# Layer 0 of a gated cross-attention network on one Trainium2 core: three neighbours change places in hand-ordered queues

## The reference

```python
x = x + tanh(g_xattn[0]) * L0_xattn(layernorm(x), ctx, ...)   # B=4, S=256, H=256, SC=1601, 16 heads, 8 groups, D=128
# in L0_xattn, for each of the 8 groups:
q  = _ln(fp8_linear(ln_out, wq));  k = _ln(fp8_linear(ln_out, wk));  v = fp8_linear(ln_out, wv)
qx = _ln(fp8_linear(ln_out, wqx)); kx, vx = split(ctx @ w_kv_x);      kx = _ln(kx)
core = softmax(q k^T / sqrt(D)) v;   xout = softmax(qx kx^T / sqrt(D)) vx
return fp8(concat(core, xout) / smooth) @ wproj.T * scale
x = x + tanh(g_ffn[0]) * L0_ffn(layernorm(x))                  # 8 experts, the best 2 weighted
```

## Time and profile before

| what | us |
|---|---|
| median of 3 runs (lowest, highest) | 1678.73 (1677.43, 1679.62) |
| the profiled execution, its own time | 1676.05 |
| its span | 1674.2 |
| TensorE busy | 1576.3 |
| VectorE busy | 1388.7 |
| ScalarE busy | 1387.7 |
| GpSimd busy | 1140.4 |
| mean granted clock of TensorE, share of full | 0.993 |

### The profile page before, as it was taken

How to read it: one execution, slowest core, us unless ns; L and a number is a source line. 1 busy time by engine, 2 the same in 40 slices (tenths; PEclk the granted TensorE clock), 3 DMA queues, 4 the chain that set the end, 5 groups by cost and what they waited for, 6 DMA issues and landing times.

```text
span 1674.2 us, 43879 instructions
## 1 busy us (share of the span) xinstructions
PE 1576.3 (94%) x15804; PEld 1000.5 (60%) x15996; DVE 1388.7 (83%) x3486; ACT 1387.7 (83%) x2346; POOL 1140.4 (68%) x1775
## 2 busy tenths in 40 slices
PE   3799999999999999999999999998898999999998
PEld 2476777767777677777777677776564333333333
DVE  7899999999999989999988999899796755655422
ACT  6688888888887888888888888775347999999997
POOL 3668778687787877888787888875775655646300
PEclk9899999999999999999999999999999999999999
DMA  4399989899899998999999999999323222222100
GB/s 180 89 199 203 196 195 198 187 208 207 207 192 201 216 212 187 216 222 217 210 193 210 213 208 209 196 190 259 97 49 114 46 51 71 43 40 47 33 14 14
DMA packets 609481, 261.12 MB, mean 156 GB/s; under 512 B 576624, under 2 KB 581744, under 8 KB 607856
## 3 DMA queue, kind: packets, MB, share of 16 engines
q1 hardware_dynamic: 605040, 258.05, 71.6%
q10 hardware_dynamic: 4224, 0.25, 0.2%
HBM read 99.15 MB, written 17.29 MB: 70 GB/s over the span
## 4 chain that ended last, share of the span: by engine, by line
PE 50%; DVE 7%; issue 4%; ACT 4%; DMA 1%; ACTq 0%; SPq 0%; DVEq 0%
PE pv L1835 9%; PE pv L2996 9%; PE score L1815 8%; PE pa L2946 4%; PE tb L1694 3%; PE tb L1735 2%; PE score L2976 2%; ACT P L2884 2%; PE tb L1794 2%; PE pa L1768 2%; PE pa L1735 1%; PE tb L2976 1%; ACT praw L2884 1%; DVE S L1298 1%; PE score L2161 1%
## 5 line engine op out<-in xcount | busy, mean ns | idle before, releaser
L1835 PE MATMUL pv<-PT,VV 128*128 128x256 bf16 (+1 forms) x2880 | 335.7, 273 | 8.0 <-DMA PT<-PB 5.9
L1569 ACT ACTIVATE PB<-S,rsum 128x1024 bf16<-128x1024 f32 (+1 forms) x256 | 246.3, 987 | 111.5 <-DVE rsum L1329 85.1
L1815 PE MATMUL score<-KK,QT 128*128 128x512 bf16 (+2 forms) x1794 | 314.3, 318 | 14.7 <-DVE mxp L1298 7.1
L1835 PEld LDWEIGHTS pv<-PT,VV 128*128 128x128 bf16 (+1 forms) x2880 | 278.2, 98 | 73.3 <-issue 34.7
L1320 DVE SCALAR_TENSOR_TENSOR PB<-S,rsum,PB 128x1024 bf16<-128x1024 f32 (+1 forms) x256 | 292.2, 1142 | 0.0
L1815 PEld LDWEIGHTS score<-KK,QT 128*128 128x128 bf16 x1920 | 157.3, 98 | 146.5 <-DVE mxp L1298 15.9
L1559 ACT ACTIVATE S<-S,nmx 128x1601 f32<-128x1601 f32 x128 | 210.1, 1642 | 5.6 <-DVE nmx L1310 5.5
L2884 ACT ACTIVATE P<-score 128x1024 f32<-128x1024 f32 x196 | 197.7, 1052 | 1.7 <-PE score L2976 0.8
L2996 PE MATMUL pv<-P,V 128*9 128x256 f32 (+1 forms) x2288 | 152.2, 380 | 1.1 <-DVE pv L2267 0.8
L1694 PE MATMUL tb<-stage,wsb 128*128 128x512 bf16 x767 | 149.0, 337 | 4.4 <-DVE stage L645 3.9
L1127 POOL TENSOR_SCALAR S<-S,rsum 128x256 f32<-128x256 f32 x128 | 74.3, 580 | 112.0 <-DVE rsum L1329 101.3
(11 more groups left out here) (295 smaller groups left out, 3656.4 us busy)
## 6 DMA issues: line engine op xcount, KB each, us to landing
x<-rs_d SPq DMA_DIRECT2D x16, 936.0 KB, 5.2
rsb<-rs_d SPq DMA_DIRECT2D x16, 936.0 KB, 5.5
wsb<-w_split SPq DMA_DIRECT2D x46, 256.0 KB, 4.6
wsb<-w_split SPq DMA_DIRECT2D x23, 512.0 KB, 5.0
wpr<-in_wprojT SPq DMA_DIRECT2D x23, 512.0 KB, 6.6
context_d<-stage SPq DMA_DIRECT2D x16, 400.2 KB, 3.9
l_ctx<-context_d SPq DMA_DIRECT2D x4, 1601.0 KB, 7.8
rawh<-in_w_all SPq DMA_DIRECT2D x12, 512.0 KB, 5.3
```

The lines of the kernel that those rows point to most:

```text
L1569: e.activation(m.PB[n % 2][:, 2 * a:a + b], m.S32[n % 2][:, a:b], ACT.Copy, scale=m.rsum[n % 2][:, 1:2]).then_inc(s["p_hi"], 1)
L1815: i = e.matmul(m.score[:, at:at + b - a], qt[:, kind, qp, q * P:(q + 1) * P], kk[:, kp, a:b], start=(k == 0), stop=(k == 2))
L1835: i = e.matmul(m.pv[:, at:at + 256], vv[0:rows, v, t, :], m.PT[k % 2][0:rows, turned(c, a), :], start=(c == first and r == 0), stop=(c == ...
```

## The change

Four edits, all to the order of work; no instruction is added or taken out.

1. VectorE: `query_stats(it+1, 0)` goes behind `scaled(4*it, 0)`.
2. TensorE: `turn_queries(it+1, 0)` (TQ0) goes from between `times_v(2*it-2, 1)` and `scores(4*it+1, 1)` to behind `keys(it+1, 2)`. `ORDER` follows; the banks stay.
3. GpSimd: in pass 32 `projection_low(30)` goes from the end of the pass to right behind the subtraction of layer 1's weights.
4. ScalarE: in pass 32 `projection_high(30)` goes in front of `act_up(0)` and `act_up(1)`.

```diff
-ORDER = tuple(w for slot in SLOTS for w in slot)
+ORDER = ("Q0", "K0", "K1", "K2", "TQ0", "K3", "Q1", "SS", "V0", "V1", "TQ1", "V2", "V3", "PR")
...
             e.tensor_tensor(m.w1[:, 1, :, :], m.l1_raw[:, :, :], m.w1[:, 0, :, :], ALU.subtract).then_inc(s["l1w_lo"], 1)
+            projection_low(NGB - 2)
...
         if it == NGB:
-            projection_low(NGB - 2)
             e.wait_ge(s["tv_done"], 4 * NGB - 2)
...
     for it in range(-1, NGB + LAG - 1):
-        query_stats(it + 1, 0)
         if it == NGB:
             dve_turned_low(e, m, s, 0)
         scaled(4 * it, 0)
+        query_stats(it + 1, 0)
...
             e.copy(m.w1[:, 0, :, :], m.l1_raw[:, :, :]).then_inc(s["l1w_hi"], 1)
+            projection_high(NGB - 2)
             act_up(e, m, s, 0)
             act_up(e, m, s, 1)
-            projection_high(NGB - 2)
...
         times_v(2 * it - 2, 1)
-        turn_queries(it + 1, 0)
         scores(4 * it + 1, 1)
         keys(it + 1, 2)
+        turn_queries(it + 1, 0)
         keys(it + 1, 3)
```

## The result

The changed kernel took **1717.39 us** (median of 4, 1714.84 to 1718.71) against 1678.55 for the kernel before on the same chip: ratio 1.0230, 95% interval 1.0217 to 1.0243. That is 38.8 us slower, and 9.1 were forecast. The direction was right; the size and the range (up to 1694) were wrong. The profiled execution took 1717.25 us with a span of 1715.4.

A forecast was written before the change was run, and what follows sets the result against it. TensorE, busy 94% of the span, was taken to bound the kernel. Terms 3.6 + 2.9 + 3.3 + 2.1 - 2.8 = +9.1 us on 1678.7 gave 1687.8 us; range 1678 to 1694.

The forecast's parts named there:

- the end: End of layer 0: projection weights ready sooner shorten TensorE's stand before `project(30)`; -2.8 us, bounds 0 and -6.9.
- VectorE's swap: Pass 8: first scaling ends 1.20 us sooner, everything behind down to `offset(32)` stays, no instruction cheaper or dearer.
- The room of the late passes: Passes from 15 on: offset ends 1.15 us before TQ0 in pass 19, so they lose nothing by TQ0's move.
- TQ0 as cover: TQ0's old place covered TensorE's wait for the offset before `scores(4*it+1, 1)`; moving it costs 0.40 us a pass.
- 9 x 0.40: Sum of the lost cover over passes 2 to 10: +3.6 us.
- The chain through GpSimd and ScalarE: Later statistics make ScalarE normalise 1.4 to 1.6 us later; hidden in pass 8, +2.9 us in passes 11 to 14.
- room for 1.35: Pass 8: ScalarE's squares of keys 3 end 1.35 us before TensorE's SS begins, so the later normalisation hides.
- 0.4 for pass 5: Pass 5: the row of key scales lands late for the swap once more, +0.4 us.
- Passes 0 and 1: Scaling waits for key scales, so statistics lose their cover; pass 0 grows 1.7, pass 1 1.6, together +3.3 us.
- Passes 11 to 14: ScalarE's later squares outlast the room before SS; passes grow 1.2, 0.8, 0.6 and 0.35, together +2.9 us.
- The stands simply go: Rival: the 6.2 us of TensorE's waits for the scaling and 2.8 at the end are won; 1669.7 us, chance 0.10.
- ScalarE becomes the bound: Rival: ScalarE's 1.4 to 1.6 us reach SS in most passes, 20 more lose 0.4 each; 1696 us, chance 0.08.

The follow-up runs named there:

- e4: The changed kernel with GpSimd's `take_magnitudes` ahead of the query normalisation: 1696.22 us, ratio 1.0107.
- e18: e4 with ScalarE normalising the first queries from pass 2 on with a constant tile, waiting for the statistics only, not GpSimd: 1690.15 us, ratio 1.0077.
- e2: The kernel before with only TensorE's TQ0 moved behind keys 2: 1683.46 us, ratio 1.0036.
- e1: The kernel before with only VectorE's query statistics moved behind the first scaling: 1711.79 us, ratio 1.0195.
- e3: The kernel before with only the two edits for the projection weights of group 30, on GpSimd and ScalarE: 1676.2 us, ratio 0.9986.
- e5: The changed kernel with VectorE's `offset(4*it)` ahead of `p_lo(4*it-1, 1)`: 1700.89 us, ratio 1.0138.
- e11: The changed kernel with `take_magnitudes` as two instructions of half the size: 1702.21 us, ratio 1.0150.
- e17: The changed kernel with `take_magnitudes` ahead of `query_norm`, offset ahead of `p_lo`, and ScalarE normalising first queries from pass 2 with a constant tile: 1682.91 us, ratio 1.0027.

## Why the prediction was wrong in size

The table has the growth of each stretch in us, from squares to squares, against the kernel before.

| passes | forecast | changed kernel | e4, no meeting | e18, nor the chain | e2, turn alone | e1, swap alone |
|---|---|---|---|---|---|---|
| 0, 1 | 3.3 | 3.3 | 3.2 | 2.1 | 0.1 | 3.6 |
| 2 to 10 | 4.0 | 13.9 | 7.3 | 5.8 | 1.9 | 13.8 |
| 11 to 14 | 2.9 | 6.2 | 4.3 | 2.4 | 2.2 | 5.3 |
| 15 to 30 | 1.7 | 18.2 | 5.4 | 3.8 | 0.1 | 11.7 |

With the end (forecast -2.8; -0.4 in the trace of the changed kernel) the first two columns give +9.1 and +41.2. How far single traces move these sums by themselves is seen in e3, whose edits touch pass 32 only: 0.9, -0.1, 1.6 and 0.1. And behind the last squares the traces of e1 and e2 are 1.7 and 1.9 us longer than the one before; they have 13.6 us at half clock in that stretch, it has 3.4 (the last few us of each trace left out).

**The step that failed** stands under "VectorE's swap": everything behind the two, down to the offset, "stays where it is", since "no instruction is cheaper or dearer". VectorE had the same work in front of it, and its work became 0.95 us longer, because what it did moved against what GpSimd did. The prediction followed GpSimd's later chain, right to its 1.14 us for the first small operation, but only on to ScalarE. It did not follow it to `take_magnitudes`, the next instruction on GpSimd. That began at 341.59; by the prediction's own 1.4 to 1.6 us it would begin at about 343.1, and `p_lo` at 343.23. e1, e4, e5 and e11 show this: 21.2 us of the traces' difference, 12.8 of them in passes 15 to 30. Some 1.3 of the 12.8 are another thing: in pass 19 the scaling of the changed kernel waits 1.50 us for the row of key scales, in e4 0.17.

**The room of the late passes.** It was rightly read as 1.15 us in pass 19, but is under 0.4 in passes 20, 25 and 30; and it was spent. In pass 23 the offset begins 26.02 us after the squares before it, against 24.18: 0.95 for the meeting, 0.64 in front of the scaling, which now waits for the row of key scales (VectorE at 886.68) that the statistics used to cover, and 0.25 in small pieces. With 1.15 of room the pass grows by 0.69, 34.05 to 34.75.

**TQ0 as cover, 0.40 a pass.** Right. From the offset's start to the next squares pass 8 takes 8.32 us before and 8.71 to 8.73 in the changed kernel, e2 and e4. In e2 VectorE regains most of it in even passes, which the 9 x 0.40 did not allow for: passes 2 to 10 grow by 1.9 us there, not 3.6.

**The chain through GpSimd and ScalarE.** The prediction had it hidden in passes 2 to 10, "room for 1.35", and worth 2.9 us behind them. The room in front of the squares was read rightly: TensorE waits for them only at the end of passes 11 and 12 in e4 (0.46 and 0.87 us). But ScalarE was late for VectorE too, with the squares of keys 1 and with the copy of the values, which VectorE takes 11.12 us after the squares in pass 9 of e4, 10.73 in e18 and 10.72 before. So "it hides" was the second step that failed. By e18 the chain costs 6.1 us in the changed order, spread over all stretches, and by e17 13.3 together with the offset's wait.

**What is left in 2 to 10**, 5.8 us against the 3.6 of TQ0's cover and 0.4 for pass 5. The scaling now stands behind VectorE's own `p_lo`, with only a short reciprocal between, and waits 0.17 us (`issue`, 22 times in the changed kernel, 3 before), which the statistics had covered. Pass 7 loses 1.7 of it (37.74 against 36.01), and I have not followed that.

**Passes 0 and 1**: 3.3 forecast, 3.3 measured, which is luck in part: pass 0 grew by 2.4 and pass 1 by 0.9, where 1.7 and 1.6 were forecast, and e3 has 0.9 of growth there without any edit to the loop. **Passes 11 to 14**: 2.9 forecast, 4.3 without the meeting. **The end**: 2.8 forecast, 1.8 by e3's medians and 1.3 in its trace, with the router held. The prediction counted the 1.65 us of the slow matmuls into the most that could be won, and the stretch at half clock only moved. In the changed kernel's own trace 0.4 us is won between the last squares and the end, and I leave open where the other 0.9 of e3's trace went.

**The rivals.** "The stands simply go" missed the same meeting. "ScalarE becomes the bound" gave 1696, which is what e4 takes, but by luck: it had the squares late for TensorE in 20 more passes, and e4 shows that at the end of two. The one that happened was not on the list: it needs GpSimd and VectorE together, and I had looked at each alone.

The Trainium skill ("SBUF — State Buffer", section "SBUF: two separate sides") says that the ports shared by VectorE and GpSimd are held exclusively by whoever starts first, for the whole instruction, and that a VectorE operation with two inputs in SBUF takes part. The prediction weighed this for the end alone. The traces agree with it in the loop too: `p_lo` reads two tensors of SBUF and is held (1.83, 1.45 and 1.35 us, by how much of GpSimd's instruction was left), the scaling, with one input in PSUM, is not (0.81). By that rule, and GpSimd's timeline 1.5 us later, a hold of about 1 us (343.1 + 1.16 - 343.23) could have been worked out beforehand. One thing in the traces doesn't go with "the whole instruction": GpSimd's power of four numbers, the first point of the last section.

## What to carry to other kernels

When an instruction moves on VectorE, shift GpSimd's dependent chain by the same amount and lay the two timelines side by side: where a GpSimd instruction of some size comes to lie on a VectorE instruction with both inputs in SBUF, one of the two may take as much longer as was left of the other (the power of a few numbers below is an exception). An instruction that reads PSUM is the cover under which GpSimd can work, and what stands behind it is as much part of the schedule as what it computes. Of two edits that are meant to help each other, measure each alone and both: the moved turn cost 5.4 us alone and saved about 7 beside the swap.

## What the runs showed of the hardware

- Not every GpSimd instruction holds `p_lo` for its whole length. The power of four numbers a partition (L1088, 1.02 us) begins 0.17 to 0.49 us ahead of a `p_lo` 59 times in the kernel before, and each of these takes its usual 0.86 to 0.87 us (640 elements) or 1.28 (1024). Pass 8 of the kernel before, GpSimd, then VectorE:

```profile
339.90 1.02 POOL L1088 TENSOR_TENSOR a_rs<-a_rs,mhalf 128x4 f32<-128x4 f32 x1
```

```profile
340.29 1.28 DVE L1320 SCALAR_TENSOR_TENSOR PB<-S,rsum,PB 128x1024 bf16<-128x1024 f32 x1
```

- At a tie GpSimd won: by the trace `p_lo` begins at 356.21 and GpSimd at 356.22, and it is VectorE that waits while GpSimd's instruction takes its usual 1.16 us. The same in pass 23, both at 891.96.
- The hold works both ways and on tiny work: four numbers a partition on GpSimd take 1.14 us behind `p_lo` instead of 0.20, a power of as few 2.06 instead of 1.02.
- A VectorE operation on 2-byte data with one tensor input is held too: `exponents` (128x512 int16) takes 1.21 us beside GpSimd's subtraction instead of 0.29. VectorE of e4, pass 9, then GpSimd:

```profile
374.70 1.21 DVE L1351 TENSOR_SCALAR ye<-yq 128x512 int16<-128x512 int16 x1
```

```profile
374.60 1.16 POOL L1101 TENSOR_TENSOR QT<-t,QT 128x512 bf16<-128x512 f32 x1
```
